# An edge and node network on one Trainium2 core: 8 rounds per loop iteration, the first layer ahead of the second, edge states updated in place

## What is computed

```python
h = jnp.maximum(_layernorm(x, axis=-1), 0.0)
x = x + _L0_gnn_ref(h, src, dst)      # degree-normalised gather by src, sum by dst
h = jnp.maximum(_layernorm(x, axis=-1), 0.0)
n = _ln(_mlp(node_feat, ...), node_enc_g, node_enc_beta)
e = _ln(_mlp(edge_feat, ...), edge_enc_g, edge_enc_beta)
for s in range(S):
    ce = jnp.concatenate([e, n[senders], n[receivers]], axis=-1)
    e = e + _ln(_mlp(ce, edge_blk_w0[s], ...), edge_blk_g[s], edge_blk_beta[s])
    agg = jax.ops.segment_sum(e.astype(jnp.float32), receivers, num_segments=num_nodes)
    cn = jnp.concatenate([n, agg.astype(n.dtype)], axis=-1)
    n = n + _ln(_mlp(cn, node_blk_w0[s], ...), node_blk_g[s], node_blk_beta[s])
return x + _mlp(n, dec_w0, dec_b0, dec_w1, dec_b1)
```

## Time and profile before

| | us |
|---|---|
| median of 3 runs | 11666.72 (11663.32 to 11670.03) |
| span of the profiled execution | 11672.6 |
| PE / PEld busy | 8130.9 / 6189.3 |
| DVE busy | 6224.5 |
| ACT busy | 5398.6 |
| POOL busy | 8560.3 |

### The profile page before, as it was taken

One profiled execution on the slowest core, in us unless ns is written; L12 is line 12 of the kernel. 1 busy time (PEld: TensorE's weight loads), 2 busy tenths in 40 slices (PEclk: granted clock), 3 DMA queues, 4 the chain that ended last, 5 costly groups with the idle time before them and its releaser, 6 DMA issues. The chain is left out here.

```text
span 11672.6 us, 199199 instructions
## 1 busy us (share of the span) xinstructions
PE 8130.9 (70%) x55867; PEld 6189.3 (53%) x55867; DVE 6224.5 (53%) x13945; ACT 5398.6 (46%) x8550; POOL 8560.3 (73%) x9018
## 2 busy tenths in 40 slices
PE   5778888888887666666666666666666666666666
PEld 4667777666665444444455545444444444444444
DVE  9988888777776444444444444433333333333333
ACT  0146666555554444444444444444444444444444
POOL 6777777777772777777777777767777777777776
PEclk8789999999998888888888888878888888888888
DMA  2322222222222333333344434432222223323332
GB/s 75 63 44 53 53 53 54 52 53 53 53 52 50 93 97 95 95 95 95 97 104 103 102 100 102 104 78 70 69 69 69 69 70 72 72 71 73 72 72 58
DMA packets 1363893, 866.26 MB, mean 74 GB/s; under 512 B 896223, under 2 KB 1049840, under 8 KB 1362557
## 3 DMA queue, kind: packets, MB, share of 16 engines
q1 hardware_dynamic: 960162, 583.07, 18.3%
q0 software_dynamic: 287776, 227.99, 12.1%
q10 hardware_dynamic: 115376, 49.25, 1.7%
HBM read 627.59 MB, written 247.78 MB: 75 GB/s over the span
## 5 line engine op out<-in xcount | busy, mean ns | idle before, releaser
L2053 POOL DMA_INDIRECT edge_blk_g<-sender_part,idx_all x6256 | 5909.0, 945 | 2157.3 <-issue 1905.3
L2107 PE MATMUL edge_blk_hps<-ident,edge_blk_g 128*128 128x128 f32 x6256 | 1214.8, 354 | 2724.2 <-DMA edge_blk_g<-sender_part,idx_all 2724.2
L157 POOL DMA_INDIRECT gather_ring<-sender_x,idx_all x2422 | 2291.4, 946 | 775.9 <-issue 771.4
L2107 PEld LDWEIGHTS edge_blk_hps<-ident,edge_blk_g 128*128 128x128 f32 x6256 | 1021.2, 247 | 3373.2 <-DMA edge_blk_g<-sender_part,idx_all 3371.9
L2195 DVE SCALAR_TENSOR_TENSOR agg<-edge_blk_aggps,vecs,agg 64x64 f32 x1564 | 442.6, 283 | 3198.3 <-PE edge_blk_aggps L2069 3034.3
L2123 ACT ACT_TABLE_LOAD x1564 | 2006.6, 1283 | 60.2 <-ACTq L1151 32.0
L2137 ACT ACTIVATE edge_blk_h<-edge_blk_hps,vecs 128x512 f32<-128x512 f32 x782 | 537.5, 687 | 2972.2 <-PE edge_blk_hps L2107 2962.5
L2090 PEld LDWEIGHTS edge_blk_yps<-w_edge_blk,edge_blk_h 128*128 128x128 f32 x6256 | 1141.7, 255 | 65.0
L2178 DVE TENSOR_REDUCE edge_blk_red<-edge_blk_sq 128x8 f32<-128x512 f32 x782 | 536.2, 686 | 1157.0 <-ACT edge_blk_sq L2129 1134.0
L2090 PE MATMUL edge_blk_yps<-w_edge_blk,edge_blk_h 128*128 128x128 f32 x6256 | 1100.0, 335 | 0.0
L1714 ACT ACT_TABLE_LOAD x782 | 1003.3, 1283 | 33.2 <-PEq L95 19.0
(11 more groups left out here) (284 smaller groups left out, 12163.1 us busy)
## 6 DMA issues: line engine op xcount, KB each, us to landing
edge_blk_e<-edge_state SPq DMA_DIRECT2D x782, 256.0 KB
edge_state<-fl_e SPq DMA_DIRECT2D x391, 256.0 KB
edge_blk_g<-sender_part,idx_all POOLq DMA_INDIRECT x6256
edge_blk_dlb<-local_dst SPq DMA_DIRECT2D x1564, 64.0 KB
edge_state<-edge_blk_new SPq DMA_DIRECT2D x391, 256.0 KB
gather_ring<-sender_x,idx_all POOLq DMA_INDIRECT x2422
edge_blk_win<-receiver_part SPq DMA_DIRECT2D x1564, 16.0 KB
fl_attr<-attr_slots SPq DMA_DIRECT2D x391, 32.0 KB
```

The lines of the kernel that those rows point to most:

```text
L157: pool.indirect_dma_start(out=gr[:, n % RING, ring_place(j), :], out_offset=None, in_=table, in_offset=bass.IndirectOffsetOnAxis(ap=idx_al ...
L2053: pool.indirect_dma_start(out=g[n % QUAD][:, i, 64 * c:64 * c + 64], out_offset=None, in_=ps_d, in_offset=bass.IndirectOffsetOnAxis(ap=idx ...
L2107: ins = nc.tensor.matmul(h_ps[n.half][:, P * i:P * i + P], g[n.b][:, i, :], ident[:, :], start=False, stop=i == TILES - 1)
```

## The change

QUAD becomes 8, so every loop body but the node loop's holds 8 rounds and every kind of transfer has 8 semaphores; the data buffers stay at four by a new BUFS (`Slot.buf`), all but the edge state `e` of the edge passes. That has eight buffers, is updated in place by `finish` (no `new`), stored from where it was loaded, and loaded again eight rounds later. The plain loop has 23 iterations instead of 47 (22 on SP in the edge passes, where the first two groups of eight stay static); the node loop keeps its 12 iterations of 16 rounds, and the number of rounds is still 391. In the edge passes PE does the first products of round n ahead of second(n-1), and sums and turns round n-4 instead of n-3; DVE makes `oha(n)` and `ohb(n-1)`, adds sums and finishes round n-5, and runs `normed` for n-2; ACT takes silu(n) before scale(n-1). `oha` gets four buffers. The order of the first pass is unchanged.

```diff
-QUAD = 4
+QUAD = 8
+BUFS = 4
...
+    def buf(self):
+        return self.b % BUFS
...
-                last = rounds_and_nodes(dve, body, count_sb, 2)
+                last = rounds_and_nodes(dve, body, count_sb)
...
         e = many(QUAD, "e", [P, CHUNK])
-        new = many(QUAD, "new", [P, CHUNK])
...
-        oha = many(2, "oha", [P, CHUNK])
+        ohb = many(BUFS, "ohb", [P, 8, WIN])
+        oha = many(BUFS, "oha", [P, CHUNK])
...
                     if keep:
-                        wait(sp, new_ok, n.back(4))
+                        landed(sp, e_out, n.back(QUAD))
+                    else:
+                        wait(sp, pre, n.back(QUAD))
                     sp.dma_start(e[n.b][:, :], edge_d[bass.ds(n.n, 1)].rearrange("a p c -> (a p) c")).then_inc(e_in[n.b], 16)
 
                 def body(n, i=None, j=None):
                     operands(n.back(2))
-                    store(n.back(6))
+                    store(n.back(8))
...
-                    if n >= QUAD:
-                        pool.wait_ge(pre, n - QUAD + 1)
+                    if n >= BUFS:
+                        pool.wait_ge(pre, n - BUFS + 1)
...
-                def body(n, i=None, j=None):
-                    sums(n.back(3))
-                    turn(n.back(3))
-                    second(n.back(1))
-                    if i is not None:
-                        nodes.pe_late(pe, i, j)
+                def first(n):
                     landed(pe, win_in, n, 32)
                     wait(pe, oha_ok, n)
...
+                def body(n, i=None, j=None):
+                    first(n)
+                    second(n.back(1))
+                    sums(n.back(4))
+                    turn(n.back(4))
+                    if i is not None:
+                        nodes.pe_late(pe, i, j)
...
                 def body(n, i=None, j=None):
-                    scale(n.back(1))
+                    silu(n, i, j)
                     if i is not None:
...
                         nodes.act_late(act, i, j)
-                    silu(n, i, j)
-                    if i is not None:
                         nodes.act_late_dma(act, i, j)
+                    scale(n.back(1))
...
                 def body(n, i=None, j=None):
-                    one_hots(n)
-                    add_sums(n.back(3))
-                    finish(n.back(3))
-                    normed(n.back(1))
+                    receivers(n)
+                    add_sums(n.back(5))
+                    one_hots(n.back(1))
+                    finish(n.back(5))
+                    normed(n.back(2))
...
-                add_sums(last.back(3))
-                finish(last.back(3))
+                add_sums(last.back(5))
+                one_hots(last.back(1))
+                finish(last.back(5))
+                normed(last.back(2))
+                add_sums(last.back(4))
+                finish(last.back(4))
                 normed(last.back(1))
-                for k in (2, 1):
+                for k in (3, 2, 1):
```

More of the change, by code:

```diff
@@ L1580, in _ @@
                 sp.wait_ge(s_at, 16 * (ATTR_PIECES + 2))
-                last = rounds_and_nodes(sp, body, count_sb, 2)
+                last = rounds_and_nodes(sp, body, count_sb)
                 for k in range(6, 0, -1):
@@ L1695, in _ @@
                 pe.wait_ge(prepared, 1)
-                last = rounds_and_nodes(pe, body, count_sb, 2)
+                last = rounds_and_nodes(pe, body, count_sb)
                 second(last.back(2))
@@ L1749, in _ @@
                 nodes.act_begin(act)
-                last = rounds_and_nodes(act, body, count_sb, 2)
+                last = rounds_and_nodes(act, body, count_sb)
                 square(last.back(2))
@@ L1921, in _ @@
                     step(v.memset(a[:, :], 0.0))
-                for b in range(QUAD):
+                for b in range(BUFS):
                     step(v.memset(gx[b][:, :, :, D + X_DIM:], 0.0))
@@ L2037, in _ @@
                     operands(last.back(k))
-                    store(last.back(k + 4))
-                for k in (4, 3, 2, 1):
+                    store(last.back(k + 6))
+                for k in (6, 5, 4, 3, 2, 1):
                     store(last.back(k))
                 if keep:
-                    for k in (4, 3, 2, 1):
+                    for k in range(QUAD, 0, -1):
                         landed(sp, e_out, last.back(k))
@@ L2106, in body @@
                     for i in range(TILES):
[L2107 removed]
+                        ins = nc.tensor.matmul(h_ps[n.half][:, P * i:P * i + P], g[n.buf][:, i, :], ident[:, :], start=False,
                                                stop=i == TILES - 1)
                     ins.then_inc(pre, 1)
[L2111 to L2112 removed]
+                def body(n, i=None, j=None):
[5 more added lines that the diff above has]
+                        nodes.pe_late(pe, i, j)
+                last = rounds_and_nodes(pe, body, count_sb)
+                for k in (4, 3, 2, 1):
                     sums(last.back(k))
                     turn(last.back(k))
[L2115 removed]
+                    if k == 4:
                         second(last.back(1))
@@ L2163, in _, with receivers @@
                 v = nc.vector
-                def one_hots(n):
-                    landed(dve, dlb_in, n, 32)
-                    wait(dve, pre, n.back(2))
-                    v.tensor_tensor(oha[n.half][:, :], dlb[n.b][:, :], keys[:, WIN:WIN + 1].broadcast_to([P, CHUNK]),
-                                    ALU.is_equal).then_inc(oha_ok, 1)
-                    v.tensor_tensor(ohb[n.b][:, :, :], keys[:, 0:WIN].rearrange("p (j w) -> p j w", j=1).broadcast_to([P, 8, WIN]),
+                def receivers(n):
+                    landed(dve, dlb_in, n, 32)
+                    wait(dve, pre, n.back(4))
+                    v.tensor_tensor(oha[n.buf][:, :], dlb[n.buf][:, :], keys[:, WIN:WIN + 1].broadcast_to([P, CHUNK]),
+                                    ALU.is_equal).then_inc(oha_ok, 1)
+                def one_hots(n):
+                    if not n.exists():
+                        return
+                    v.tensor_tensor(ohb[n.buf][:, :, :], keys[:, 0:WIN].rearrange("p (j w) -> p j w", j=1).broadcast_to([P, 8, WIN]),
                                     loc_all[:, bass.ds(n.n * 8, 8)].rearrange("p (j w) -> p j w", w=1).broadcast_to([P, 8, WIN]),
```

87 lines of the change are left out of this document (41 added, 46 removed).

## The result

| | before | changed |
|---|---|---|
| median of 4 runs | 11666.53 (11663.32 to 11670.03) | 11777.76 (11768.24 to 11796.32) |
| span of the profiled execution | 11672.6 | 11794.5 |

The changed kernel is slower: ratio 1.0098, 95% interval 1.0084 to 1.0112. The forecast was 11724 with a range to 11765; the direction is right, and the loss of 111 us is nearly twice the 57 that was forecast.

The account below looks back on a forecast made before the run. POOL's gathers were taken to bound the edge passes and DVE the first pass. Loop turns -12.4, fetch stops +58.3 and tails +11 sum to +57 us on 11666.7, so 11724, range 11668 to 11765.

Parts of the forecast that it names:

- Bound and edge rounds (0): Edge passes: POOL's gathers are the limit, so the shorter chain round PE, ACT and DVE saves 0.
- Stop at the back-edge (22 x 2.65 = 58.3): First pass, plain loop: DVE's body of 289 instructions is fetched anew at each of 22 branches back, +58.3 us.
- 289 is nearer to 345: Reason given that DVE's plain body of 289 instructions is not held: 149 was held, 345 not, and 345 is nearer.
- some 90 (22 turns of four): First pass, plain rounds: instruction packets in the trace rise from 6 to some 90.
- DVE is the limit here and has no slack, so each lands in the time: 22 x 2.65: First pass: each fetch stop of DVE adds its 2.65 us to the time, +58.3 us in all.
- 46 (58.3 - 12.4): First pass: the stretch of plain rounds gets about 46 us longer, fetch stops less the saved loop turns.
- PE then waits for DVE's one-hots: First pass: PE's body grows too, but PE waits for DVE at a stop, so no cost was added for PE.
- The 0.27 us a turn (-12.4, or -6.5 with the body held): First pass: 46 loop turns of 0.27 us go, -12.4 us; if DVE's body is held, only 24 go, -6.5 us.
- Tails (+11): Ends of the edge passes: more rounds of sums and `normed` follow the last gather, +6 and +5 us.
- that the body is held (0.19): Rival for the first pass: DVE's 289 instructions are not fetched anew, +5 us in all, 11671; chance 0.19.
- Rival 4: First pass: each turn costs two fetches, 22 x 5 = +110 us, some 11,775 with the rest; chance 0.03.
- Rivals 2 and 3: Edge passes: faster if chain-bound, some 10,420, chance 0.02; slower if POOL waits for late `pre`, 12,100, chance 0.03.

Follow-up runs that it names:

- the runs with 26 and 28 memsets: The changed kernel with 26 or 28 one-column memsets on DVE ahead of the first pass: 11846.7 and 11660.2 us, one run each.
- the run of the edge passes alone: The changed kernel with the first pass put back to 4 rounds a body: 11688.6 us, ratio 1.0017 to the kernel before.
- the run with 40 memsets: The changed kernel with 40 one-column memsets on DVE ahead of the first pass: 11666.8 us, ratio 1.0007 to the kernel before.
- 16 memsets: The changed kernel with 16 one-column memsets on DVE ahead of the first pass: 11777.3 us, ratio 1.0101 to the kernel before.

## Why the prediction was half right

- **Bound and edge rounds (0):** right. POOL's gathers kept their pace, and the shorter chain had nothing to win.
- **Stop at the back-edge (22 x 2.65 = 58.3):** right in place, count and size: 22 times 2.62. The place decides whether a body is held, as the runs with 26 and 28 memsets show at the front end of a packet; that only the last five or six instructions reached into a fourth one stays the count it was called, since no run sits at that edge. "289 is nearer to 345" was no reason at all: 357 instructions were held where they lay in three packets. The 85 instruction packets met the forecast "some 90 (22 turns of four)" by luck: the stretch from 1030 to 1990 us has 16 turns, so (85 - 6) / 16 is 5 packets a turn.
- **The failed step: "DVE is the limit here and has no slack, so each lands in the time: 22 x 2.65".** The plain rounds became 108 us longer where 46 (58.3 - 12.4) were forecast: a turn cost 5.4 us. The stop idles PE for 3.63 us, PE's clock halves, and PE hands the slower sums and lookup back to DVE. The prediction left PE at "PE then waits for DVE's one-hots", as if a waiting engine came back unchanged. The run with PE kept busy shows the mechanism; 22 x 5.4 - 12.4 = +106 against +108 measured. The kernel before had it to read, behind the very stop that the prediction quotes: the 16 matmuls of the sums take 2.61 us there, the transposes 1.06, and DVE waits 1.75 and 0.53 for them. I priced the idle time of DVE and didn't read on, on PE:

```profile
2461.65 2.61 PE L1638 MATMUL fl_aggps<-fl_ohb,fl_gx 128*96 128x64 f32 x16 [1.92 <-DVE fl_ohb L1774]
2464.05 1.06 PE L1658 MATMUL fl_tps<-ident,fl_t 128*128 128x128 f32 x4
...
2464.39 0.28 DVE L1835 SCALAR_TENSOR_TENSOR agg<-fl_aggps,sum_g,agg 96x64 f32 x1 [1.75 <-PE fl_aggps L1638]
2465.20 0.28 DVE L1835 SCALAR_TENSOR_TENSOR agg<-fl_aggps,sum_g,agg 96x64 f32 x1 [0.53 <-DVE agg L1835]
```

- **The 0.27 us a turn (-12.4, or -6.5 with the body held):** right; with the body in three packets the plain rounds are 6 to 8 us shorter by the traces.
- **Tails (+11):** under-priced by a little: 17 in the changed kernel's profile, 16 in the run of the edge passes alone, 13 to 16 in the traces with memsets or fillers. The order on DVE was counted right, but two things were missed. PE's first sums behind the last gathered terms now stand behind the second layer, so DVE's first addition starts 2.7 us after the end of those terms (7779.03 + 2.08 to 7783.85) instead of 1.3 (7680.60 + 2.08 to 7683.99). And the last rounds of add_sums don't overlap `normed` as I assumed; behind 3.14 us of idle time PE's sums take 1.12 us instead of 0.69 here too, at a granted clock of 0.50. One addition of the kernel before, then of the changed one PE's last gathered terms, DVE's additions, PE's later sums, and a stretch with its clock:

```profile
7683.99 0.70 DVE L2195 SCALAR_TENSOR_TENSOR agg<-edge_blk_aggps,vecs,agg 64x64 f32 x2 [9.07 <-PE edge_blk_aggps L2069]
...
7779.03 2.08 PE L2108 MATMUL edge_blk_hps<-ident,edge_blk_g 128*128 128x128 f32 x8 [6.65 <-DMA edge_blk_g<-sender_part,idx_all]
...
7783.85 0.28 DVE L2207 SCALAR_TENSOR_TENSOR agg<-edge_blk_aggps,vecs,agg 64x64 f32 x1 [9.64 <-PE edge_blk_aggps L2075]
...
7789.32 0.70 DVE L2207 SCALAR_TENSOR_TENSOR agg<-edge_blk_aggps,vecs,agg 64x64 f32 x2 [1.11 <-issue]
...
7793.81 0.70 DVE L2207 SCALAR_TENSOR_TENSOR agg<-edge_blk_aggps,vecs,agg 64x64 f32 x2 [1.11 <-issue]
...
7795.92 0.70 DVE L2207 SCALAR_TENSOR_TENSOR agg<-edge_blk_aggps,vecs,agg 64x64 f32 x2 [0.63 <-PE edge_blk_aggps L2075]
...
7798.51 0.70 DVE L2207 SCALAR_TENSOR_TENSOR agg<-edge_blk_aggps,vecs,agg 64x64 f32 x2 [0.90 <-PE edge_blk_aggps L2075]
...
7790.17 0.69 PE L2075 MATMUL edge_blk_aggps<-edge_blk_ohb,edge_blk_t 128*64 128x64 f32 x16 [2.03 <-DVE agg L2207]
...
7794.66 1.12 PE L2075 MATMUL edge_blk_aggps<-edge_blk_ohb,edge_blk_t 128*64 128x64 f32 x16 [3.14 <-DVE agg L2207]
...
7794.00:7799.00 5.00, 4.28 (x40) 3.34 (x40) 2.79 (x8) 0.00 (x0) 0.00 (x0) 0.50 0.24 93
```

From the first to the second addition it is 5.5 us, then 4.5, 2.1 and 2.6, where the rows of before gave 2.17 for a round without `normed`. A `normed` between two additions costs 2.3 to 3.3 and not half of 2.0.
- **Not seen:** the node rounds' gain of 17 us. Its cause is open; PE's second stop is gone there, but no run shows that this pays for it.
- **Rivals:** that the body is held (0.19) would have given 11,671; the run with 40 memsets is that case, and it came at 1.0007. Rival 4's 11,775 lies 3 us from the measured time by coincidence: its mechanism, two fetches a turn, is not what happened (one stop of 2.6 us and as much again from the clock); it is seen only with 26 memsets. Rivals 2 and 3 are out by POOL's 800 gathers per 1000 us.

## What to carry to other kernels

Behind a stall, read on through the next round of every engine that waited for it: here DVE's stop idled PE, PE's clock halved, and the echo was as long as the stop. Before unrolling a loop further, count where the body lies, and check its back-edge for an idle time with no releaser and a rise of instruction fetches; a body of 289 instructions cost 5.4 us a turn, 7.2 or nothing, by where it began. A stop costs only where its engine is the limit: DVE's node loop of edge pass 1 stops 11 times with 16 memsets and never with 28, and POOL's gathers take 3905 us from the first to the last in both. And a shorter chain in a stage in which another engine never waits is worth nothing, while its longer tail is paid at every pass.

## Not expected of the hardware

- Filler work on PE made the kernel 0.35% faster: six us at half clock are dearer than 12 matmuls that compute nothing.
- Two memsets that do nothing moved the plain rounds of the first pass by 154 us (two single executions, 11846.7 against 11660.2 in all), and a body that by my count begins on the last place of a packet stops for 4.9 us a turn, not 2.6.
- DVE's loop of 357 instructions went round in 0.27 us from place 14 or 15 of a packet, and in 2.8 to 3.0 us from places 30 to 54 and 116.
